# Attention: score matmuls in four column groups of 32 keys, in place of one of 128

## The reference

```python
q, k, v = ...                      # 4 sequences, 16 heads, 1024 tokens, 16 per head
scores = jnp.einsum('bhqd,bhkd->bhqk', q, k) * hs ** (-0.5)
p = jax.nn.softplus(scores)
p = p * p
p = p * jnp.tril(jnp.ones((t, t)))               # causal: a query sees keys up to its own
attn = p / (jnp.sum(p, axis=-1, keepdims=True) + 1e-09)
out = jnp.einsum('bhqk,bhkd->bhqd', attn, v)
```

## Time and profile before

| | |
|---|---|
| three runs, us | 1607.56 median, 1599.33 to 1610.26 |
| the profiled execution, us | 1605.87, its span 1604.0 |
| attention phase in the span | from about 276 to 626 us, 16 passes |
| one pass | 21.3 us |
| granted clock of PE, mean of the span | 0.99 |
| DMA engines, busy share from 293 to 603 us | 0.70 |

### The profile page before, as it was taken

The page is one execution under the profiler, slowest core; times in us unless marked ns, Lnnn a source line. Parts: engine busy times, 40 slices in busy tenths (PEclk is TensorE's granted clock), DMA queues, the critical chain, the costliest instruction groups (busy, mean ns, idle before and its releaser), DMA issues. The chain is left out here.

```text
span 1604.0 us, 28965 instructions
## 1 busy us (share of the span) xinstructions
PE 1520.9 (95%) x11188; PEld 1125.0 (70%) x11188; DVE 1216.4 (76%) x2334; ACT 873.0 (54%) x1372; POOL 411.4 (26%) x382
## 2 busy tenths in 40 slices
PE   8999898999999998999989999979999999899998
PEld 7888776444444446888867778756777777678777
DVE  4554797898999986664578888768777777688886
ACT  3333387988888886332332222278888887321220
POOL 0002111222122224100433221113555555211111
PEclk9999999999999999999999999999999999999999
DMA  4000065777777750000100000022333333100000
GB/s 159 26 1 14 20 188 178 100 95 106 106 101 102 100 72 2 14 1 1 40 27 8 1 1 1 1 69 78 102 101 107 106 107 107 40 14 27 14 27 27
DMA packets 57160, 95.83 MB, mean 60 GB/s; under 512 B 7904, under 2 KB 29632, under 8 KB 57024
## 3 DMA queue, kind: packets, MB, share of 16 engines
q1 hardware_dynamic: 56064, 93.38, 26.4%
q10 hardware_dynamic: 960, 0.59, 0.1%
HBM read 76.91 MB, written 17.04 MB: 59 GB/s over the span
## 5 line engine op out<-in xcount | busy, mean ns | idle before, releaser
L1438 DVE TENSOR_TENSOR att_weights<-att_weights 128x1024 f32<-128x1024 f32 (+1 forms) x224 | 267.7, 1241 | 39.4 <-ACT att_weights L1411 39.1
L928 DVE SCALAR_TENSOR_TENSOR X<-ps,moe_gsel,X 128x256 f32<-128x256 f32 x512 | 246.1, 483 | 63.5 <-PE ps L48 41.1
L1411 ACT ACTIVATE att_weights<-ps 128x1024 f32<-128x1024 f32 (+1 forms) x288 | 264.9, 992 | 39.8 <-PE ps L1347 20.5
L48 PE MATMUL ps<-w_experts_hi,moe_xh 128*128 128x512 f32 x512 | 205.1, 401 | 1.1 <-DVE X L928 1.1
L48 PE MATMUL ps<-w_experts_hi,moe_xl 128*128 128x512 f32 x512 | 203.3, 397 | 0.0
L48 PE MATMUL ps<-w_experts_lo,moe_xh 128*128 128x512 f32 x512 | 201.6, 394 | 0.0
L1367 PE MATMUL ps<-att_weights,att_v_ones 64*32 64x64 f32 (+5 forms) x2048 | 157.6, 400 | 0.0
L424 ACT ACTIVATE ffn_gates<-ps,ffn_gate_bias 128x512 f32<-128x512 f32 x72 | 49.5, 688 | 148.3 <-PE ps L48 126.6
L48 PEld LDWEIGHTS ps<-w_experts_hi,moe_xh 128*128 128x128 f32 x512 | 96.2, 188 | 27.9 <-DVE X L928 4.5
L48 PEld LDWEIGHTS ps<-w_experts_lo,moe_xh 128*128 128x128 f32 x512 | 96.1, 188 | 22.1
L48 PEld LDWEIGHTS ps<-w_experts_hi,moe_xl 128*128 128x128 f32 x512 | 96.3, 188 | 20.3
(11 more groups left out here) (281 smaller groups left out, 3672.1 us busy)
## 6 DMA issues: line engine op xcount, KB each, us to landing
ssm_lb<-decays SPq DMA_DIRECT2D x32, 512.0 KB, 4.7
ssm_rise<-decays SPq DMA_DIRECT2D x28, 512.0 KB, 3.9
qk_parts<-qkv_part SPq DMA_DIRECT2D x32, 384.0 KB, 2.8
q_stack<-qk_parts SPq DMA_DIRECT2D x64, 128.0 KB, 4.6
k_stack<-qk_parts SPq DMA_DIRECT2D x64, 128.0 KB, 7.8
att_q_stack<-qk_parts SPq DMA_DIRECT2D x64, 128.0 KB, 4.8
att_k_stack<-qk_parts SPq DMA_DIRECT2D x64, 128.0 KB, 8.8
out<-X SPq DMA_DIRECT2D x7, 512.0 KB, 2.9
```

What stands on the lines that cost most here:

```text
L48: ins = pe.matmul(out, l(k), r(k), start=first and n == 0, stop=last and n == len(passes) - 1)
L928: dve.scalar_tensor_tensor(out=x, in0=ring[:, e // 2, (e % 2) * C:(e % 2 + 1) * C], scalar=gsel[:, s, j, e:e + 1], in1=x, op0=ALU.mult, op ...
L1411: act.activation(Wt[:, u % WU, 0:n], scores(u)[:, 0:n], ACT.Softplus).then_inc(p_done, 1)
L1438: dve.tensor_tensor(wt, wt, wt, ALU.mult).then_inc(sq_done["dve"], 1)
```

## The change

Every score matmul and every mask is cut into groups of 32 keys, each with weights of 128 rows by 32 columns and an output in its own 32 partitions. A REST segment becomes four matmuls and only its last two groups are masked; an UPPER piece becomes two; the UPPER bank's fill becomes four, with 128 rows instead of 64. The matmul that cleared the output bank is gone: the first REST values of block 0 start the accumulation themselves.

```diff
@@ -1281,6 +1281,7 @@
     SU, WU = 3, 12
+    KG = 32
...
@@ -1333,18 +1334,21 @@
                 if upper:
-                    low = slice(0, HALF)
                     pe.sem_inc(scores_free, 1)
-                    for r in range(2):
-                        pe.matmul(scores(u)[r * HALF:(r + 1) * HALF, 0].rearrange("p (s q) -> p s q", q=HALF), neg[low, low],
-                                  ident16[low, low].unsqueeze(1).broadcast_to([HALF, BANK // HALF, HALF]), start=True, stop=False)
+                    for g in range(P // KG):
+                        at = g * KG % HALF
+                        pe.matmul(scores(u)[g * KG:(g + 1) * KG, 0].rearrange("p (s q) -> p s q", q=HALF), neg[:, at:at + KG],
+                                  ident16[:, 0:HALF].unsqueeze(1).broadcast_to([P, BANK // HALF, HALF]), start=True, stop=False)
                 for n, (h, kj, t, c, q, w, part) in enumerate(segments):
-                    rows = slice(h % 2 * HALF, (h % 2 + 1) * HALF) if part == UPPER else slice(0, P)
-                    keys = slice(kj * P, kj * P + (HALF if part == UPPER else P))
-                    ins = pe.matmul(scores(u)[rows, t, c:c + w], SK[s][:, h, keys], SQ[s][:, h, q:q + w],
-                                    start=not upper, stop=n >= len(segments) - 2 if upper else part == FULL)
+                    groups = range(h % 2 * HALF, (h % 2 + 1) * HALF, KG) if part == UPPER else range(0, P, KG)
+                    for g in groups:
+                        keys = kj * P + (g % HALF if part == UPPER else g)
+                        masked = part == REST and g >= HALF
+                        ins = pe.matmul(scores(u)[g:g + KG, t, c:c + w], SK[s][:, h, keys:keys + KG], SQ[s][:, h, q:q + w],
+                                        start=not upper, stop=n >= len(segments) - 2 if upper else not masked)
                     if part == REST:
-                        ins = pe.matmul(scores(u)[:, t, c:c + HALF], neg[:, :], ident16[:, HALF:P], start=False, stop=True)
+                        for g in range(HALF, P, KG):
+                            ins = pe.matmul(scores(u)[g:g + KG, t, c:c + HALF], neg[:, g:g + KG], ident16[:, HALF:P], start=False, stop=True)
...
                     pe.wait_ge(o_done, (i * 2 + s) * BLOCKS + qb + 1)
-                    if qb == 0:
-                        pe.matmul(O(qb), ident16[:, :], neg[:, 0:1].broadcast_to([P, BANK]), start=True, stop=False)
...
                     ins = pe.matmul(O(qb)[h * 2 * HD:(h + 1) * 2 * HD, q0:q0 + w], values,
-                                    Wt[rows, (s * PU + unit) % WU, t, c:c + w], start=kj == 0 and part == FULL, stop=part == UPPER and kj == (qb + 1) * GT - 1)
+                                    Wt[rows, (s * PU + unit) % WU, t, c:c + w], start=kj == 0 and part != UPPER, stop=part == UPPER and kj == (qb + 1) * GT - 1)
```

## The result

The changed kernel takes 1625.4 us in the median of 4 runs (1623.9 to 1631.0), against 1606.2 of before, also in 4: a ratio of 1.013, 95% interval 1.009 to 1.017, so slower by 19 us. The forecast was 1636, the range 1592 to 1672.

The account below looks back on a forecast made before the run. PE was taken to set the 21.3 us pass, DVE and ACT close behind. PE work of 18.6 plus 4.4 us of instruction stalls made 23.0; over all passes, with the clock, +29 us: 1636 us, range 1592 to 1672.

Parts of the forecast that it names:

- Blocks of 256 instructions, late behind the stack loads: PE's instruction queue q8: the next 16 KB block waits behind the stack-load burst; some 26 blocks more in the phase.
- The gain in PE's own work: PE in each attention pass: fewer shape switches 1.58 us, no clearing matmul 0.21, UPPER scores 0.07; together 1.87 us less.
- What a pass takes without supply trouble: Attention pass without instruction stalls: DVE needs 19.2 us, ACT 18.9, so about 19.7 us, 1.6 less than before.
- The size of the stalls: PE waiting for instruction blocks in passes with a burst: mean 4.4 us a pass, 3 to 6 as bounds.
- the rival with smaller stalls: Blocks get between stack packets sooner: stalls of 1.5 to 2.5 us, passes 20.5 to 21.5, 1595 to 1612 us; chance 0.17.
- The four positions of the block bounds that I walked: One pass stepped through with four placements of the instruction-block bounds: stalls of 3.6, 4.3, 4.9 and 4.9 us.
- the walk: Stepping through a pass by estimated block waits: asked for at 5.5 us, begun 11, there 14.3, needed 11.2.
- The clock: PE's granted clock falls at times behind the new stalls: 5 us more for all passes, between 0 and 25.
- The sum: Passes with a burst take 23.0 us against 21.3: 15 x 1.7 = +26, last pass gains 1.6, clock 5; together +29.
- Supply is no limit: Rival: instruction supply stalls nothing, the gain is had, a pass takes 19.7 us, the time 1582 us; chance 0.14.
- Something still costlier: Rival: matmuls of 32 keys obstruct each other or instruction intake is slow, 25 ns each: 1668 to 1683 us; chance 0.08.

## Why the prediction was right, and where its terms were off

The direction, the place and the mechanism were as forecast, and 1636 against 1625.4 is in the range. Point by point:

- **Blocks of 256 instructions, late behind the stack loads.** Shown: q8 has 26 blocks more in the span and 27 in the phase (forecast some 26); the stalls stand whole blocks apart and end 2.8 to 3.5 us behind a block's beginning (I had 3.3 in the burst's second half), and they go with the burst while the traffic stays. "In every pass with a burst, 3 to 5 us" was too much: of the 15 passes the first has none, four more have 0.5 to 1.0 us, and the others 1.5 to 5.3.
- **The gain in PE's own work.** Forecast 1.87 us a pass. Between the two kernels without loads a usual pass has 20.64 and 18.80 us of busy PE, 1.84 us less, and 15 passes 307.95 and 281.61, 1.76 a pass. Groups do run beside each other.
- **What a pass takes without supply trouble.** Forecast 19.7 us; 20.35 came. The step was "DVE then needs 19.2 and ACT 18.9": I looked at busy sums and not at the order of DVE's work. Its copy stands behind a square at 7 units' lag, PE's transposes at 2, and a PE that is 1.8 us faster gets there first. With the later transposes it is 19.89. Also PE didn't set the pass of before alone; it was coupled to ACT by the wait of the earlier trace rows, so 0.21 us off PE left the pass at 21.27.
- **The size of the stalls, mis-sized.** Forecast 4.4 us a pass, and 3 to 6 as the forecast's bounds; measured 39.0 / 15 = 2.6, between them and the 1.5 to 2.5 of the rival with smaller stalls, whose 1595 to 1612 us were too low all the same. The four positions of the block bounds that I walked gave 3.6 to 4.9; in the real passes the stalls run from none to 5.3, and only four have more than 4. Part of it is seen. In nine cases PE enters a block on leaving one stall and runs dry into the next. These blocks lasted 6.0 to 7.9 us (here from 356.64 to 362.59), where the walk had 5.7, so they covered more of the wait. The wait itself was as walked: the next block's load began 4.0 to 7.7 us behind the entry (walk 5.5), and PE went on 2.9 to 3.4 us later (walk 3.3). The rest isn't settled.
- **The clock, mis-sized the other way.** Forecast 5 us more for all passes, with 25 as the bound. In the 15 passes PE was busy at the lower level for 32.7 us, for 9.3 in the kernel before and 5.7 in the changed kernel without loads. Half of each is what the level cost: 16.4, 4.7 and 2.9 us, so 12 us more than before. PE is busy 301.0 us where the same instructions without loads take 281.6; of these 19.4 us the clock is 13.5, and the cause of the other 5.9 isn't shown. I had one row behind one stall, of 2.57 us, and took it for rarer than it is.
- **The sum.** 18.6 + 4.4 = 23.0 us a pass was forecast and 23.15 measured, with other parts: 18.8 of work (as without loads), 0.9 of clock, 0.4 of longer PE busy time with no cause shown, 2.6 of stalls, 0.45 of waits for ACT and DVE. That the pass agrees is luck: too much stall cancels what was left out. Of the 10.6 us between 1636 and the median about 7 are an error in the sum: I counted +1.7 us a pass from a pass without stalls (21.3), though the profiled execution has 21.56 with them, 4 us in 15 passes, and I added 5 us of clock on top, while the 23.15 us hold the clock's cost already; the 0.15 us a pass by which the forecast was short take 2 back. The rest lies outside the 15 passes: they are 23.8 us longer, the last pass is 1.3 shorter, the spans differ by 21.0 and the medians by 19.2, and the median of before is now 1606.2, not 1607.6.
- **The rivals.** "Supply is no limit" had 1582 us. It was wrong for the kernel as changed, and right as a condition: with the supply mended the same PE code runs at 1585.5 (loads left out) and 1587.7 us (loads spread), and at 1578.5 with the transposes a step later and a load a unit. That the fetch is "mostly hidden" (the Trainium skill, "Runtime: NRT & Kernel Launch", Instruction fetch mechanics) holds in the changed kernel only without a burst: one stall of 0.3 us against 39.0 us. "Something still costlier" didn't come: passes of 19.89 us with some 1006 instructions in each are 20 ns an instruction, under the 25 ns that it rested on.

## What to carry to other kernels

Count the instructions of an engine, not only its busy time: a change that cuts matmuls into four makes PE use up its blocks of instructions faster (2.3 to 3.9 in a pass here), and a block must last about as long as the wait for the next one. Beside bursts of some 15 us, blocks of 8 to 9 us nearly covered it here (3.9 and 4.7 us of stalls in 15 passes), and blocks of 5 to 6 us didn't (39.0). Where a loader issues many DMAs at once, spread them by what the compute has finished; here that alone turned +19 us into -18. And when the bounding engine gets faster, go through the orders of the engines that are nearly as busy, since what was just in time is now late.

## What the runs showed of the hardware that I had not expected

The stack burst from 348 to 362 us let one block of instructions through after 6 us and the next only at its end, although PE had entered its last one at 356.6 us. Behind a stall that ended near or after the end of a burst the next block's load began 1.0 to 1.5 us after PE had gone on (13 of 14 cases, once 2.2). The clock did not follow the length of a stall alone: over the next 3 us it was 0.66 after a stall of 2.25 us, 1.00 after 2.66, 0.71 after 2.57, 0.56 after 3.38, and 0.50 after 3.36 and 4.5 us. At 0.50, 3 us hold 1.5 us of PE's work at the full clock, so behind these two stalls PE lost at least 1.5 us each beside their own length. And values in some column groups start while masks still run in others: the row of two values at 396.43 us begins before the masks of 396.54 and 396.65.

```profile
396.43 0.57 PE L1369 MATMUL ps<-att_weights,att_v_ones 128*32 128x448 f32 x2
396.54 0.21 PE L1351 MATMUL ps<-ident,neg 128*32 128x64 bf16 x2
```
